# A decaying scan over 128 rows: from a TensorE product to four shifted additions on VectorE

## What is computed

```python
# layer 1
h     = rmsnorm(layernorm(x), g_res) @ W_in.T + b_in
u     = exp(-0.001) * rmsnorm(ctx, g_init)[:, :512]
s[k]  = a * s[k-1] + u[k]                   # a first-order scan over the rows k, a = exp(-dt), dt = -log(1-exp(-0.001))
plug  = clip(cumsum(marks at cumsum(patch_lens)-1) - 1, 0, 511)
x     = x + s[plug] + h
# layer 2
y     = layernorm(x);  y_prev = y shifted by one token
r     = sigmoid((mu_r*y + (1-mu_r)*y_prev) @ W_r.T)
k     = relu((mu_k*y + (1-mu_k)*y_prev) @ W_k.T) ** 2
out   = x + r * (k @ W_v.T)
```

## Time and profile before

| what | value |
|---|---|
| median of 3 runs | 780.18 us (779.64 to 780.68) |
| the profiled execution | 780.35 us, of which the span from the first to the last instruction is 778.8 us |
| TensorE busy | 755.4 us, 97% of the span |
| VectorE busy | 556.2 us, 71% |
| ScalarE busy | 413.7 us, 53% |
| GpSimd busy | 175.5 us, 23% |
| transfers | 85.73 MB, 110 GB/s over the span |
| TensorE's granted clock, mean | 0.992 of full speed |

### The profile page before, as it was taken

One profiled execution on the slowest core, in us unless ns is written; L12 is line 12 of the kernel. 1 busy time (PEld: TensorE's weight loads), 2 busy tenths in 40 slices (PEclk: granted clock), 3 DMA queues, 4 the chain that ended last, 5 costly groups with the idle time before them and its releaser, 6 DMA issues.

```text
span 778.8 us, 10909 instructions
## 1 busy us (share of the span) xinstructions
PE 755.4 (97%) x3462; PEld 621.9 (80%) x3463; DVE 556.2 (71%) x1005; ACT 413.7 (53%) x682; POOL 175.5 (23%) x175
## 2 busy tenths in 40 slices
PE   7878899999999999999999999999999999999997
PEld 4656688888888888888888888888888888888876
DVE  6797886766858677686776769577676967667552
ACT  4346565554546655455664545556454655544760
POOL 6622131313102131220313122131311213130000
PEclk9999999999999999999999999999999999999999
DMA  8556170524417053350705326071531706140011
GB/s 311 147 192 178 41 215 3 153 105 109 149 42 216 0 128 128 88 169 37 213 7 122 135 69 187 14 194 50 121 135 47 209 0 185 72 108 15 1 54 55
DMA packets 42765, 85.73 MB, mean 110 GB/s; under 512 B 3536, under 2 KB 3536, under 8 KB 42704
## 3 DMA queue, kind: packets, MB, share of 16 engines
q1 hardware_dynamic: 30768, 63.74, 21.8%
q0 software_dynamic: 9216, 16.78, 13.6%
q10 hardware_dynamic: 2736, 4.73, 1.8%
HBM read 64.26 MB, written 21.76 MB: 110 GB/s over the span
## 4 chain that ended last, share of the span: by engine, by line
PE 88%; DVE 4%; DMA 2%; issue 2%; ACT 2%; POOL 1%; SPq 0%; DVEq 0%; ACTq 0%; POOLq 0%
PE bank L494 28%; PE bank L495 28%; PE bank L496 28%; PE bank L599 3%; DMA xt<-in_x_turned 1%; POOL ring L433 1%; DMA s_rows<-scanned 1%; DMA ctx_rows<-in_ctx 1%; DVE ring L1034 1%; DVE xk_lo L908 1%; DVE scratch L1004 0%; DVE gate L1062 0%; ACT scratch L809 0%; DVE bn_a L937 0%; ACT scratch L807 0%
## 5 line engine op out<-in xcount | busy, mean ns | idle before, releaser
L433 POOL DMA_INDIRECT ring<-s_rows,patch_now x60 | 101.7, 1695 | 262.7 <-DMA s_rows<-scanned 231.0
L908 DVE TENSOR_TENSOR xr_lo<-scratch,xr_hi 128x512 fp32r<-128x512 f32 x124 | 85.6, 690 | 70.3 <-ACT xr_hi L715 69.8
L1004 DVE SCALAR_TENSOR_TENSOR scratch<-turned,cols,scratch 128x512 f32<-128x512 f32 x128 | 94.5, 749 | 31.5 <-ACT scratch L764 24.9
L715 ACT ACTIVATE turned<-bank 128x512 f32<-128x512 f32 x64 | 33.2, 604 | 137.1 <-PE bank L599 133.5
L494 PE MATMUL bank<-wi_hi,xt_hi 128*128 128x512 f32 x256 | 102.1, 399 | 3.3 <-DVE xt_lo L908 2.7
L494 PE MATMUL bank<-xk_hi,wk_hi 128*128 128x512 f32 x256 | 100.1, 391 | 3.4 <-DVE xk_lo L908 3.4
L494 PE MATMUL bank<-wr_hi,xr_hi 128*128 128x512 f32 x256 | 99.7, 390 | 1.0 <-DVE xr_lo L908 1.0
L495 PE MATMUL bank<-wi_lo,xt_hi 128*128 128x512 f32 x256 | 100.4, 392 | 0.0
L496 PE MATMUL bank<-wi_hi,xt_lo 128*128 128x512 f32 x256 | 100.2, 391 | 0.0
L496 PE MATMUL bank<-xk_hi,wk_lo 128*128 128x512 f32 x256 | 99.6, 389 | 0.0
L495 PE MATMUL bank<-xk_lo,wk_hi 128*128 128x512 f32 x256 | 99.6, 389 | 0.0
(11 more groups left out here) (134 smaller groups left out, 1283.4 us busy)
## 6 DMA issues: line engine op xcount, KB each, us to landing
ring<-in_x SPq DMA_DIRECT2D x16, 1024.0 KB, 7.4
out<-gate SPq DMA_DIRECT2D x64, 256.0 KB, 2.1
xt<-in_x_turned SPq DMA_DIRECT2D x14, 1024.0 KB, 5.2
ctx_rows<-in_ctx SPq DMA_DIRECT2D x16, 512.0 KB, 8.0
s_rows<-scanned ACTq DMA_DIRECT2D x16, 256.0 KB, 2.4
gate<-in_L_xattn_W_in SPq DMA_DIRECT2D x4, 256.0 KB, 6.2
xt<-in_x_turned SPq DMA_DIRECT2D x2, 512.0 KB, 8.0
ring<-in_x_turned SPq DMA_DIRECT2D x1, 1024.0 KB, 12.9
```

Of the source, the lines that this page charges most:

```text
L433: pool.indirect_dma_start(ring[b.slot][:, t, :], None, s_rows[:, :], bass.IndirectOffsetOnAxis(ap=rows, axis=0), compute_op=ALU.add).then_ ...
L715: return nc.scalar.activation(to, of, ACT.Copy)
L908: return nc.vector.tensor_tensor(to, whole, high, ALU.subtract)
L1004: nc.vector.scalar_tensor_tensor(scratch[:, 2 + i % 2, :], turned[:, c, 1:S + 1], cols[:, 1 + which, c:c + 1], scratch[:, i % 2, :], ALU.m ...
```

## The change

The batches 2 to 15 no longer use TensorE for the scan. Since `a` is tiny, the scan is written as four steps with doubling reach: with `shift(v, k)` the rows of `v` moved down by `k` partitions and zeros above, step n is `v = shift(v, k) * a**k + v` for k = 8, 4, 2, 1. A partition shift is done by a transfer from SBUF to SBUF into a new buffer `above`, split in two: 112 rows, and the remaining 16 - k. A step is one `scalar_tensor_tensor` on VectorE; after the last, `add_bias` adds the bias. The eight transfers of a batch are issued by SyncE's queue, which now loads context, tokens and transposed tokens in this order. `u_high` and `u_low` of these batches go. TensorE loses the scan's product and, in `turn`, its waits for `s_copied` and `far_over`; these stand within the far branch. Batches 0 and 1 keep the product.

```diff
+def shift_steps(powers):
+    return [(k, powers[k] if k < len(powers) else 0.0) for k in (8, 4, 2, 1)]
...
+    STEPS, MOST = len(steps_of_scan), P - 16
...
         @block.sync
+            def shift_scan(b):
+                since = b.plus(-2)
+                for n, (k, _) in enumerate(steps_of_scan):
+                    if n == 0:
+                        reached(sp, u_ready, b, 1, 1)
+                    else:
+                        reached(sp, earlier_added, since, STEPS, n)
+                    of = scanned if n else u
+                    sp.dma_start(above[k:k + MOST, :], of[0:MOST, :]).then_inc(earlier_loaded, 16)
+                    sp.dma_start(above[k + MOST:P, :], of[MOST:P - k, :]).then_inc(rest_loaded, 16)
...
                 if new.exists(B) and not is_first(new, 1):
+                    reached(sp, far_over, new.plus(-1), 1, 1)
                     rows_added(sp, new.plus(-1))
-                    reached(sp, xt_lo_ready, new.plus(-1), 2, 2)
-                    load_xt(new)
+                    load_ctx(new)
                     reached(sp, out_ready, b.plus(-1), T, T)
...
                     load_x(new)
-                    reached(sp, far_over, new.plus(-1), 1, 1)
-                    load_ctx(new)
+                    reached(sp, xt_lo_ready, new.plus(-1), 2, 2)
+                    load_xt(new)
+                    shift_scan(new)
...
         @block.tensor, turn(b)
-                    if t == SCAN and b.plus(1).exists(B) and not is_first(b):
-                        reached(pe, s_copied, b.plus(1), 1, 1)
-                        reached(pe, far_over, b.plus(1), 1, 1)
...
                 if new.exists(B):
-                    scan(new)
                     far(new)
...
         @block.scalar, iteration(b)
-                    u_high(new)
...
         @block.vector
+            def clear_head(b):
+                reached(dve, earlier_added, b.plus(-2), STEPS, 0)
+                nc.vector.memset(above[0:steps_of_scan[0][0], :], 0.0).then_inc(head_zeroed, 1)
+            def scan_step(b, n):
+                since = b.plus(-2)
+                reached(dve, earlier_loaded, since, 16 * STEPS, 16 * (n + 1))
+                reached(dve, rest_loaded, since, 16 * STEPS, 16 * (n + 1))
...
+                nc.vector.scalar_tensor_tensor(scanned[:, :], above[:, :], steps_of_scan[n][1], (scanned if n else u)[:, :],
+                                               ALU.mult, ALU.add).then_inc(earlier_added, 1)
+            def add_bias(b):
+                reached(dve, earlier_added, b.plus(-2), STEPS, STEPS)
+                nc.vector.tensor_tensor(scanned[:, :], scanned[:, :], bias[:, :], ALU.add).then_inc(s_copied, 1)
...
                 if is_first(b):
+                    clear_head(new)
...
-                    u_low(new)
+                    scan_step(new, 0)
                     norm_b(nxt)
                     gating(b, 0)
                     gating(b, 1)
+                    scan_step(new, 1)
                     x_lo(new, 0)
                     x_lo(new, 1)
-                    scan_out(new)
+                    scan_step(new, 2)
+                    add_out(b, 0)
+                    add_out(b, 1)
+                    scan_step(new, 3)
+                    add_bias(new)
                     far(new)
...
-                        if m == 2:
-                            scan_input(new)
+                        if m in (2, 3):
+                            scan_step(new, m - 2)
...
-                    u_low(new)
                 if b.exists(B):
                     gating(b, 0)
                     gating(b, 1)
                 if new.exists(B):
-                    scan_out(new)
+                    scan_step(new, 2)
+                if b.exists(B):
+                    add_out(b, 0)
+                    add_out(b, 1)
+                if new.exists(B):
+                    scan_step(new, 3)
+                    add_bias(new)
                     far(new)
```

More of the change, by code:

```diff
@@ L162, in build @@
         patch_now = sb("patch_now", [P, T], U32)
+        above = sb("above", [P, D])
         def part(row, start, shape, dt):
@@ L531, in far @@
                         else:
-                            reached(pe, s_copied, b, 1, 1)
+                            if b.fixed and b.number() < 2:
+                                reached(pe, s_copied, b, 1, 1)
+                            pe.wait_ge(far_u_lo, earlier * T + 1)
                         product(scan_bank(b)[:, :], decay_hi[:, 1, :], decay_lo[:, 1, :], u_hi[:, :], u_lo[:, :],
                                 True, False).then_inc(far_carried, 1)
-                        pe.wait_ge(far_u_lo, done)
+                        pe.wait_ge(far_u_lo, earlier * T + c + 1)
                         product(scan_bank(b)[:, :], decay_hi[:, 0, :], decay_lo[:, 0, :], u_hi[:, :], u_lo[:, :],
                                 False, True).then_inc(far_s, 1)
+                    pe.wait_ge(far_copied, earlier * (T - 1) + T - 1)
+                    hold(pe, pe_passed)
             def gate_product(b):
@@ L959, in scan_input @@
                 reached(dve, rs_c_done, b, 1, 1)
-                reached(dve, u_lo_ready, b.plus(-1), 1, 1)
+                if b.fixed and b.number() < 3:
+                    reached(dve, u_lo_ready, b.plus(-1), 1, 1)
+                else:
+                    reached(dve, earlier_added, b.plus(-3), STEPS, STEPS)
                 nc.vector.scalar_tensor_tensor(u[:, :], ctx_rows[:, 0:D], rs_c[:, :], g_ctx[:, :],
                                                ALU.mult, ALU.mult).then_inc(u_ready, 1)
+            def clear_head(b):
[5 more added lines that the diff above has]
+                reached(dve, rest_loaded, since, 16 * STEPS, 16 * (n + 1))
+                if n == 0:
+                    reached(dve, head_zeroed, since, 1, 1)
+                    reached(dve, s_stored, b, 16, 0)
+                    reached(dve, u_ready, b, 1, 1)
+                else:
+                    reached(dve, earlier_added, since, STEPS, n)
+                nc.vector.scalar_tensor_tensor(scanned[:, :], above[:, :], steps_of_scan[n][1], (scanned if n else u)[:, :],
[3 more added lines that the diff above has]
+                nc.vector.tensor_tensor(scanned[:, :], scanned[:, :], bias[:, :], ALU.add).then_inc(s_copied, 1)
             def far(b):
@@ L968, in far @@
                     earlier = far_earlier(dve, b)
+                    if b.fixed and b.number() < 2:
+                        reached(dve, s_done, b, 1, 1)
+                    nc.vector.tensor_copy(u_hi[:, :], u[:, :]).then_inc(far_u_hi, 1)
+                    dve.wait_ge(far_u_hi, earlier * T + 1)
+                    low(u_lo[:, :], u[:, :], f32(u_hi[:, :])).then_inc(far_u_lo, 1)
+                    dve.wait_ge(far_u_lo, earlier * T + 1)
                     for c in range(1, T):
@@ L1132, in iteration @@
                     norm_b(nxt)
+                if new.exists(B):
+                    scan_input(new)
                 for m in range(C):
```

15 lines of the change are left out of this document (6 added, 9 removed).

## The result

The changed kernel takes **807.41 us** (median of 4 runs, 806.26 to 808.18) against 779.91 (4 runs, 779.61 to 780.68) before: ratio 1.036, interval 1.0343 to 1.0374. The forecast was 773.3 with a range up to 782.0, so both the sign and the range were wrong. The profiled execution took 806.73 us.

The account below looks back on a forecast made before the run. TensorE, busy for 97% of the span, was taken as the bound; 780.35 - 8.84 (13 products) + 2.0 (first changed iteration) = 773.5 us profiled, 773.3 us for the median, range 770.5 to 782.0.

Parts of the forecast that it names:

- The bound and the gain: Steady part: TensorE, busy without gaps, loses one product of 0.68 us per batch, 13 x 0.68 = 8.84 us gained.
- What hides VectorE's work and the moved loads: VectorE's 2.3 us more per batch fit its idle time; later loads keep 1.4 us to spare; both priced at nothing.
- R = 2.1: Time from a VectorE scan step's end, through a shift transfer, to the next step's start: 2.1 us, within 2.0 to 2.6.
- The formula around R: Steady batches: the bias ends at 410.44 + 3R; TensorE waits only if R is over 2.24, then 3 us per us.
- `s_copied` to the projection: ScalarE, after the bias: 0.36 for the store's issue and 0.60 for the first copy before TensorE's next projection can start.
- Iteration 0: First changed iteration, with its own order: a whole round trip of 2.1 in the open, ending 2.0 us later than before.
- Rival 2: Scan round trips at the slow end, 2.57 us, decide the batch: 12.9 us in 13 batches, 786.2, slower; chance 0.14.
- Rival 3: Next batch's loads come late if gathers land 1.4 us later; 1 us over costs 13 us, 786; chance 0.08.

Follow-up runs that it names:

- two steps: The changed kernel with only the scan steps by 2 and 1, without those by 8 and 4 and their transfers: 771.31 us, 0.9895.
- the work without its trips: The changed kernel with steps by 2 and 1, the other two replaced by the same instruction with factor 0 and no transfer: 773.36 us, 0.9911.
- the steps earlier: The changed kernel with all four steps and eight transfers, only VectorE's order differing so that steps stand earlier: 771.66 us, 0.9879.
- three steps: The changed kernel with only the scan steps by 4, 2 and 1, without the step by 8: 773.23 us, 0.9911.
- the orders alone: The kernel before, product kept, with the new load order and, in the loop, `u` and output additions 0 and 1 earlier: 779.85 us, 1.0.
- the store moved away: The changed kernel with the scan store of batches 2 to 15 issued by SyncE's queue behind the shifts, instead of ScalarE's: 787.96 us, 1.011.

## Why the prediction was wrong, step by step

- **The bound and the gain: right.** TensorE is the bound, and a batch without its product and without a new wait takes 45.29 us, as forecast; four kernels show it (two steps, the work without its trips, the steps earlier, and two batches of three with three steps).
- **What hides VectorE's work and the moved loads: right.** The two added steps without their trips leave the batch at 45.28 to 45.29 us, and the orders alone leave the time where it was.
- **R = 2.1: wrong, and this is the step that failed.** It took the output stores as the nearest relative "since queue and neighbours are the same" and let the small transfer end first. Measured: 2.86 to 2.93 in the batch shown, and over 3.2 for the first trip in every third batch. A store of 256 KB (a seventh more than the 112 rows, not an eighth) is no measure for a transfer between two SBUF tiles (0.3 us more) of 112 partitions (0.3 more), and with the small transfer, which ends last, a trip is 0.2 to 0.3 longer still. The bounds of 2.0 to 2.6 missed it too, as both ends were rows of transfers to HBM.
- **The formula around R: right.** In the batch shown: three trips of 8.69 us against 3 x 2.24 make 1.97 us late. Steps of 0.69 instead of 0.75 give back 0.18. Step 0 ends 384.47 - 375.45 = 9.02 ahead of the transposes' start, where (417.13 - 0.68) - 407.50 = 8.95 were counted, which gives back 0.07; the bias starts 0.04 late. That leaves 1.76.
- **`s_copied` to the projection: 0.32 short.** Counted were 0.36 for the store's issue and 0.60 for a copy. Measured from 386.94 to 388.22 are 1.28, as the copies begin 0.18 behind the issue (387.30 to 387.48) and the rest passes before the matmul starts. Together 2.08 us; the projection starts 388.22 - 384.47 - 1.67 = 2.08 late.
- **Iteration 0: the place was right.** Forecast was a projection 2.7 us late (2.0 and the 0.68). By the same count it is 99.30 - 93.07 - 1.67 = 4.56 late. Of the 1.9 more, the open trip with its step is 0.70 (2.86 for 2.1, 0.69 for 0.75), the way from `s_copied` 0.24 (98.10 to 99.30 for 0.96), and step 2 comes 0.37 later behind the gatings than counted, since its own trip outlasts the low parts of `xt` (it waits 0.59). The other 0.6 is no lateness of the scan: the gatings end 1.02 us earlier than before (89.67 for 90.69), but TensorE reaches the transposes 2.30 earlier (93.07 for 95.37), and only 0.68 of that was counted. Its stretch at the lower clock, 1.6 us, is gone there, and a wait of 0.70 for a low part stands in its place. The half clock behind the late projection was not in the sum.
- **Rival 2 is what happened.** Its mechanism, place and price (3 us for each us of R) hold; its R of 2.57 was still too small, and its chance of 0.14 too low for a quantity that no row showed and whose threshold lay 0.14 above the value taken.
- **Rival 3 was next in line.** The longest wait of the steady part, 3.02 us at 436.80, has a part of it: in that batch ScalarE waited for its transposed tokens, and step 0 ended 8.12 us ahead of the transposes (423.75 to 431.87) instead of 9.02. A first trip of 3.21 us instead of 2.86 is the rest. The wait of ScalarE:

```profile
413.82 2.02 ACT L740 ACTIVATE xt_hi<-xt 128x1024 fp32r<-128x1024 f32 x2 [1.88 <-DMA xt<-in_x_turned]
```

It comes in four steady batches of the change. With the store moved away it comes 14 times, 40.3 us in all (one of them, 7.2 us, at the start, where the kernel before has it too).

The Trainium skill's fit (DMA: Bandwidth & Descriptors, "Anatomy of one DMA"), given for the software path, pointed to the right side: an estimate of 2.53 us for 112 rows against 2.7 measured. Its law does not hold for these transfers, which SyncE and ScalarE issue. By it the 128 rows would land later, at 2.60, and they land in 2.3 between SBUF tiles and in 2.0 to HBM. The measurements decide.

## What to carry to other kernels

A chain of transfers that VectorE has to wait for in turn is priced by its own kind of transfer. If the trace has none, the threshold says how sure one must be: here 0.14 us of error in one trip, three times a batch, decided over sign and size. The remedy was an earlier start in the program (step 0 ends 11.7 us ahead of the transposes instead of 9.0), not a shorter transfer: work that is off the bound engine costs nothing only if its end, too, comes before that engine asks for it. And before a store goes into a queue, look at what stands behind it there.

## What was not expected of the hardware

- 112 partitions between SBUF tiles land later than 128 (2.6 against 2.3 us). By the semaphore updates in the trace the first of the 16 comes after 2.15 us in both; the last comes after 2.31 with 128 partitions and 2.58 with 112 (medians of steps 0 and 1). Why was not tried.
- Issuing 8 to 15 rows takes longer than issuing 112: 0.71 to 0.84 us against 0.52 to 0.58 on SyncE's queue. Issuing the small transfer from a second queue did not shorten the change's time.
- Indirect gathers land later when the loads of 2.5 MB overlap them: 9.7 us in the median instead of 5.0 with the store on the same queue.
- TensorE's clock fell to its lower level behind the waits of 4.32 and 2.22 us, but not behind that of 3.02 (1.00 in 436 to 440); in the kernel before it fell behind waits of 0.39 to 0.85. The length of a wait alone does not tell. What does stays open.
